# Indirect writes of expert rows: add to the zeroed scratch tensor, or overwrite it

## The chip, the cores and the metric

The kernel runs on one core of one Trainium2 chip. The metric is the device time of one execution in microseconds (us); the lower, the better. The time before is the median of three runs.

## What is computed

The input x holds 16 sequences of 256 tokens with 128 features: 4096 tokens. It is layer-normalised to xn, and the output is x plus two branches of xn: a gated recurrence (a causal convolution of four taps, two sigmoid gates, a scan along the sequence, a projection and an RMS norm) and a mixture of eight experts. Only the second is touched here:

```python
probs = softmax(xf @ Wr);  eidx = argmax(probs);  p_tok = probs[eidx]
rank  = position of the token among those of its expert;  keep = rank < cap    # cap = 4096 / 8 = 512
xe = xf[dispatch]                                   # expert e: its (up to) 512 rows
h  = maximum(einsum('ecd,edf->ecf', xe, W1), 0.0)
ye = einsum('ecf,efd->ecd', h, W2)
ye = ye * (pe * valid)[:, :, None]
y  = zeros((t, d)).at[dispatch.reshape(-1)].add(ye.reshape(E * cap, d))
return x + recurrence(xn) + y
```

Each token has one expert, so a row of y gets at most one row of ye. A token beyond the capacity of its expert gets zero.

## The kernel before

The work is written by hand as one instruction list for each engine, with semaphores between them. It has three stretches.

**Routing.** x is loaded, normalised and written to the scratch tensor `xn_rows` in DRAM (line 296, SP's queue). The router's logits give `idx_in` (which token stands in which expert slot) and `idx_out` (to which row of `y_rows` the result of a slot goes). For a slot without a token `idx_out` names a row of its own in the second half of `y_rows`, which nobody reads. The first half (4096 rows) is filled with zeros by four DMAs on SP's queue (line 300), since the rows of dropped tokens are read later though no slot writes them.

**Experts.** There are 8 experts with 4 tiles of 128 rows each, 32 tiles in all. GpSimd (POOL) issues for each tile a gather (line 366: 128 rows of 512 bytes from `xn_rows` into the tile of `xn_tok`, called `gathered`) and later a scatter (line 373: the 128 result rows of the tile to the rows of `y_rows` that `idx_out` names). POOL's order is `gather(0)` to `gather(3)`, then `scatter(e)` and `gather(e + 4)` in turn for e = 0 to 3, and then `scatter(4)` to `scatter(7)`. `scatter(e)` waits until VectorE (DVE) has copied the expert's output out of PSUM into the same tiles (`evict`, line 940, and tile by tile at line 945 for expert 7). Before its first scatter, POOL waits on `idx_done` and on `zero_out`, which counts the four zero fills. TensorE (PE) transposes the gathered rows (`turn`, line 512), and runs the up products (lines 525 to 527) and the down products (line 538). ScalarE (ACT) and DVE run the recurrence, cut into stages, between the steps of the experts. SP loads the weights of expert e once the gathers of expert e - 2 have landed (line 305).

**End.** SP waits until all 32 scatters have landed (`scattered` at 16 x 32), and issues eight loads of `y_rows` (line 309). ACT or DVE multiplies these rows by the token's probability (lines 719, 988), DVE adds the rest (lines 988, 993), and eight stores on the queues of SP and ACT write the output (lines 312, 724).

Of the kernel before, what the change touches and what calls it, by code (L numbers as in the profile page):

```python
# [9 lines left out]
ALU = mybir.AluOpType  # L10
# [4 lines left out]
B, L, D = 16, 256, 128  # L15
# [28 lines left out]
def rglru_moe_kernel(nc, x, params, gamma, weights, xn_rows, y_rows, out):  # L44
# [14 lines left out]
    with ExitStack() as ctx:  # L59
# [6 lines left out]
        def sem(name):  # L66
            return ctx.enter_context(nc.semaphore(name))
# [63 lines left out]
        gathered = xn_tok  # L131
# [100 lines left out]
        scattered = sem("scattered")  # L232
# [53 lines left out]
        @block.sync  # L286
        def _(sp):
            for u, (t0, nt) in enumerate(UNITS):
                if u not in ACT_UNITS:
                    sp.dma_start(tiles(x_tok, t0, nt), tile_rows(x_rows, t0, nt)).then_inc(x_in[u], 16)  # L290
            for e in range(2):
                sp.dma_start(w_raw[:, e, :], weights[:, e * WW:(e + 1) * WW]).then_inc(w_in[e], 16)
            sp.dma_start(gam[:, :], gamma.partition_broadcast(P)).then_inc(gam_in, 16)
            for u, (t0, nt) in enumerate(UNITS):
                normalised(sp, (t0 + nt) // 4 - 1)
                sp.dma_start(own_rows(xn_rows, t0, nt), tiles(xn_tok, t0, nt)).then_inc(xn_out, 16)

            sp.wait_ge(zeroed, 1)
            for c in range(C):
                sp.dma_start(y_rows[c * TC:(c + 1) * TC, :].rearrange("(p j) d -> p (j d)", p=P),  # L300
                             zeros).then_inc(zero_out, 16)

            for e in range(2, E):
                sp.wait_ge(gather_in[e - 2], 16 * ST)
                sp.dma_start(w_raw[:, e, :], weights[:, e * WW:(e + 1) * WW]).then_inc(w_in[e], 16)

            sp.wait_ge(scattered, 16 * NS)
            for n in range(NH):
                sp.dma_start(tiles(ybuf, 4 * n, 4), own_rows(y_rows, 4 * n, 4)).then_inc(y_in[n], 16)
            for n in range(0, NH, 2):  # L310
                sp.wait_ge(final_done, n + 1)
                sp.dma_start(tile_rows(out_rows, 4 * n, 4), tiles(ybuf, 4 * n, 4)).then_inc(stored, 16)
            sp.wait_ge(stored, 16 * NH)

        @block.gpsimd
        def _(pool):
            g = nc.gpsimd
            exact = dict(allow_small_or_imprecise_dtypes=True)
            g.memset(eps[:, 0:1], LN_EPS).then_inc(eps_done, 1)
            g.memset(eps[:, 1:2], RMS_EPS).then_inc(eps_done, 1)  # L320
            g.memset(eps[:, 2:3], 0.25).then_inc(eps_done, 1)
            g.memset(ident[:, :], 0.0).then_inc(fill, 1)
            g.memset(ones[:, :], 1.0).then_inc(fill, 1)
            g.memset(later[:, :], 0.0).then_inc(fill, 1)
            pool.wait_ge(fill, 1)
            g.affine_select(out=ident[:, :], in_=ident[:, :], compare_op=ALU.not_equal, fill=1.0, base=0,
                            pattern=[[-1, P]], channel_multiplier=1).then_inc(ident_done, 1)

            pool.wait_ge(fill, 3)
            g.affine_select(out=later[:, :], in_=later[:, :], compare_op=ALU.is_ge, fill=-1.0, base=0,  # L330
                            pattern=[[1, P]], channel_multiplier=-1).then_inc(consts, 1)
            g.iota(tok_id[:, :], [[1, NT]], base=-T // 2, channel_multiplier=NT, **exact).then_inc(consts, 1)
            g.iota(block_id[:, :, :], [[P, ST], [0, NT]], base=0, channel_multiplier=0, **exact).then_inc(consts, 1)
            g.iota(slot_in[:, :], [[P, ST]], base=0, channel_multiplier=1, **exact).then_inc(consts, 1)
            g.iota(spare[:, :, :], [[CAP, E], [P, ST]], base=T // 2, channel_multiplier=1,
                   **exact).then_inc(consts, 1)

            def normalise(u):
                t0, nt = UNITS[u]
                pool.wait_ge(nmr_done, u + 1)  # L340
                for t in range(t0, t0 + nt):
                    if t in POOL_TILES:
                        g.tensor_scalar(xn_tok[:, t * D:(t + 1) * D], x_tok[:, t * D:(t + 1) * D], rstd[:, t:t + 1],  # L343
                                        nmr[:, t:t + 1], ALU.mult, ALU.add).then_inc(norm_pool, 1)

            def number(part):
                v0, v1 = part * P // 4, (part + 1) * P // 4
                g.iota(values[:, v0:v1, :], [[1, P // 4], [0, NT]], base=v0, channel_multiplier=0,
                       **exact).then_inc(valued, 1)

            for part in range(4):
                number(part)
            normalise(0)
            normalise(1)
            normalise(2)
            normalise(3)
            pool.wait_ge(par_in, 16)
            pool.wait_ge(ident_done, 1)
            for k in range(TAPS):
                g.tensor_scalar(diag[:, k, :], ident[:, :], par[:, CONV_W + k:CONV_W + k + 1], 0.0, ALU.mult,  # L360
                                ALU.add).then_inc(diag_done, 1)
            normalise(4)

            def gather(e):
                for s in range(e * ST, (e + 1) * ST):
                    g.indirect_dma_start(gathered[:, s * D:(s + 1) * D], None, xn_rows,  # L366
                                         bass.IndirectOffsetOnAxis(ap=idx_in[:, s:s + 1], axis=0)
                                         ).then_inc(gather_in[e], 16)

            def scatter(e):  # L370
                for s in range(e * ST, (e + 1) * ST):
                    pool.wait_ge(y_done, s + 1 if e == E - 1 else ST * (e + 1))
                    g.indirect_dma_start(y_rows, bass.IndirectOffsetOnAxis(ap=idx_out[:, s:s + 1], axis=0),  # L373
                                         gathered[:, s * D:(s + 1) * D], None).then_inc(scattered, 16)

            pool.wait_ge(xn_out, 16 * NU)
            pool.wait_ge(xn_tp, NH)
            pool.wait_ge(idx_done, 1)
            AHEAD = 4
            for e in range(AHEAD):  # L380
                gather(e)
            pool.wait_ge(idx_done, 2)
            pool.wait_ge(zero_out, 16 * C)
            for e in range(E):
                scatter(e)
                if e + AHEAD < E:
                    gather(e + AHEAD)
# [637 lines left out]
```

## Time and profile before

| | us |
|---|---|
| device time, three runs | 145.51, 145.52, 144.76 |
| median | 145.51 |
| span of the profiled execution | 153.7 |
| from the start of the last scatter's issue to the end of that span | 18.6 |

The only time shown of the profiled execution is its span, from the first to the last instruction. It is 8.2 us longer than the median of the runs, which were taken without the profiler; a row of the trace stands for a share of 153.7 us. The page gives the busy time of each engine, then the span in 40 equal slices of 3.84 us, the DMA queues, the chain of work that ended last, and the costliest groups of instructions by line. The bar of an indirect DMA on POOL is the time in which POOL builds the transfer's descriptors; the move of the data comes after it. The timeline gives, in square brackets, how long the engine stood idle before the instruction, and what ended that.

### The profile page before, as it was taken

To read this page: it belongs to the slowest core of one execution; us is meant where nothing else is said; L and a number is where in the kernel's file an instruction comes from. 1 tells how busy PE (TensorE), PEld (TensorE's weight loads), DVE (VectorE), ACT (ScalarE), POOL (GpSimd) and SP (SyncE) were. 2 spreads that over 40 slices of the span, in tenths; PEclk is the share of its full clock that TensorE was granted. 3 is DMA by queue.
4 is the path that set the end of the run, shared out by engine and by line. 5 is a ranking of instruction groups with operands and counts; after the bars stand their busy time and mean duration, and the time that the engine had idled before them with its cause. 6 is when DMAs were issued, how large, how long until landed. Compare 5 with 4: busy or idle time off the path is not lost.

```text
span 153.7 us, 2064 instructions
## 1 busy us (share of the span) xinstructions
PE 111.9 (73%) x676; PEld 89.6 (58%) x676; DVE 96.8 (63%) x213; ACT 91.3 (59%) x207; POOL 87.2 (57%) x104
## 2 busy tenths in 40 slices
PE   5594988990999759979989382999999999400000
PEld 5494976730478437936936272798989979400000
DVE  6474779898699610183143014998989189972770
ACT  3262897561388255948935397484959859620560
POOL 8924570088777737737777720797977746640000
PEclk9999999999599987999999997599999999955555
DMA  3997339711643641115116110001111111117996
GB/s 111 305 339 271 134 143 399 286 32 36 187 116 113 188 143 64 51 34 171 55 51 188 51 34 0 31 25 37 31 48 42 51 36 53 34 34 251 327 337 178
DMA packets 14346, 19.27 MB, mean 125 GB/s; under 512 B 1664, under 2 KB 10112, under 8 KB 14336
## 3 DMA queue, kind: packets, MB, share of 16 engines
q1 hardware_dynamic: 8464, 12.91, 25.7%
q0 software_dynamic: 2048, 4.20, 9.0%
q10 hardware_dynamic: 3824, 2.04, 4.8%
q8 instruction: 5, 0.08, 0.2%
q14 instruction: 5, 0.04, 0.1%
HBM read 10.76 MB, written 8.39 MB: 125 GB/s over the span
## 4 chain that ended last, share of the span: by engine, by line
PE 43%; DMA 15%; ACT 14%; DVE 9%; issue 5%; POOL 4%; another core or an unknown queue 4%; SPq 1%; POOLq 1%; ACTq 1%; DVEq 0%
PE bank L472 10%; DMA x_tok<-in_x 8%; PE bank L538 7%; PE bank L527 5%; PE bank L525 5%; PE bank L526 5%; DMA dec<-y_rows 4%; ACT sq L687 4%; PE bank L404 3%; POOL xn_tok L366 3%; DVE sca L955 2%; PE bank L512 2%; DMA y_rows<-xn_tok,idx_out 2%; DMA xn_tok<-xn_rows,idx_in 2%
## 5 line engine op out<-in xcount | busy, mean ns | idle before, releaser
L373 POOL DMA_INDIRECT y_rows<-xn_tok,idx_out x32 | 36.1, 1128 | 24.1 <-DVE xn_tok L940 14.5
L366 POOL DMA_INDIRECT xn_tok<-xn_rows,idx_in x32 | 36.0, 1125 | 18.0 <-issue 9.4
L538 PE MATMUL bank<-w_raw,h_sb 128*128 128x128 f32 x256 | 30.5, 276 | 2.6 <-issue 1.6
L538 PEld LDWEIGHTS bank<-w_raw,h_sb 128*128 128x128 f32 x256 | 29.4, 192 | 2.9 <-issue 1.8
L674 ACT ACTIVATE h_sb<-bank 128x512 f32<-128x512 f32 x32 | 19.2, 599 | 15.4 <-PE bank L527 11.5
L472 PE MATMUL bank<-xc,par 128*128 128x512 f32 x32 | 17.9, 687 | 4.0 <-ACT dec L649 4.0
L525 PE MATMUL bank<-xg_hi,w_hi 128*128 128x512 f32 x32 | 16.9, 529 | 3.7 <-DVE xg_lo L905 3.6
L871 DVE TENSOR_TENSOR w_lo<-w_raw,w_hi 128x512 fp32r<-128x512 f32 x8 | 5.5, 682 | 15.1 <-issue 13.2
L905 DVE TENSOR_TENSOR xg_lo<-bank,xg_hi 128x512 fp32r<-128x512 f32 x8 | 5.5, 691 | 14.3 <-ACT xg_hi L668 10.5
L527 PE MATMUL bank<-xg_hi,w_lo 128*128 128x512 f32 x32 | 13.7, 430 | 0.0
L526 PE MATMUL bank<-xg_lo,w_hi 128*128 128x512 f32 x32 | 13.7, 429 | 0.0
L472 PEld LDWEIGHTS bank<-xc,par 128*128 128x128 f32 x32 | 6.0, 204 | 11.0 <-issue 10.9
L898 DVE SCALAR_TENSOR_TENSOR xc<-xnT,par,xc 128x1020 f32<-128x1020 f32 (+2 forms) x9 | 11.5, 1277 | 0.3
L525 PEld LDWEIGHTS bank<-xg_hi,w_hi 128*128 128x128 f32 x32 | 7.0, 218 | 7.4 <-DVE xg_lo L905 4.2
L343 POOL TENSOR_SCALAR xn_tok<-x_tok,rstd,nmr 128x128 f32<-128x128 f32 x16 | 7.5, 479 | 6.6 <-DVE nmr L767 6.6
L649 ACT ACTIVATE dec<-bank,half_b 128x512 f32<-128x512 f32 x8 | 5.2, 685 | 9.4 <-PE bank L472 4.6
L687 ACT ACTIVATE sq<-bank 128x128 f32<-128x128 f32 x32 | 8.8, 275 | 1.9 <-PE bank L552 1.2
L719 ACT ACTIVATE dec<-dec,prob 128x128 f32<-128x128 f32 x16 | 5.1, 391 | 8.1 <-DMA dec<-y_rows 8.0
L933 DVE TENSOR_TENSOR_SCAN xnT<-dec,inp 128x256 f32<-128x256 f32 x16 | 9.7, 672 | 0.0
L955 DVE SCALAR_TENSOR_TENSOR sca<-bank,rms,gam 128x128 f32<-128x128 f32 x32 | 9.0, 345 | 0.3
L922 DVE SCALAR_TENSOR_TENSOR inp<-inp,xc 128x512 f32<-128x512 f32 x8 | 5.2, 692 | 5.5 <-ACT inp L649 5.5
L526 PEld LDWEIGHTS bank<-xg_lo,w_hi 128*128 128x128 f32 x32 | 7.0, 219 | 2.7 <-issue 1.5
(118 smaller groups left out, 212.4 us busy)
## 6 DMA issues: line engine op xcount, KB each, us to landing
w_raw<-in_weights SPq DMA_DIRECT2D x8, 512.0 KB, 9.0
y_rows<-sca SPq DMA_DIRECT2D x4, 512.0 KB, 4.9
dec<-y_rows SPq DMA_DIRECT2D x8, 256.0 KB, 4.9
xn_rows<-xn_tok SPq DMA_DIRECT2D x3, 512.0 KB, 2.6
x_tok<-in_x SPq DMA_DIRECT2D x2, 512.0 KB, 7.5
out<-dec SPq DMA_DIRECT2D x4, 256.0 KB, 3.6
out<-dec ACTq DMA_DIRECT2D x4, 256.0 KB, 3.5
x_tok<-in_x ACTq DMA_DIRECT2D x1, 512.0 KB, 12.0
```

Of the source, the lines that this page charges most:

```text
L366: g.indirect_dma_start(gathered[:, s * D:(s + 1) * D], None, xn_rows, bass.IndirectOffsetOnAxis(ap=idx_in[:, s:s + 1], axis=0)).then_inc(g ...
L373: g.indirect_dma_start(y_rows, bass.IndirectOffsetOnAxis(ap=idx_out[:, s:s + 1], axis=0), gathered[:, s * D:(s + 1) * D], None).then_inc(s ...
L472: mm(gate[n % 2][:, :], par[:, w:w + D], xc[:, c * TC + (i % 2) * HT:c * TC + (i % 2 + 1) * HT], start=True, stop=True).then_inc(gate_mm, 1)
L525: mm(b, w_hi[:, e % 2, w], xg_hi[:, :], start=True, stop=False)
L526: mm(b, w_hi[:, e % 2, w], xg_lo[:, :], start=False, stop=False)
L527: mm(b, w_lo[:, e % 2, w], xg_hi[:, :], start=False, stop=True).then_inc(h_mm, 1)
L538: last = mm(tile_of(e, s), h_sb[:, k * CAP + s * P:k * CAP + (s + 1) * P], w_raw[:, e, F + k * D:F + (k + 1) * D], start=(k == 0), stop=(k ...
L674: a(h_sb[:, k * CAP:(k + 1) * CAP], hbank[n % 3][:, :], ACT.Relu).then_inc(h_done, 1)
L687: a(sq[:, :], obank[n % 3][:, i * D:(i + 1) * D], ACT.Square, accum_out=ssq[:, t:t + 1]).then_inc(ssq_done, 1)
L898: ins = v.scalar_tensor_tensor(dst[:, :, back:], src[:, :, 0:L - back], par[:, k:k + 1], dst[:, :, back:], ALU.mult, ALU.add)
L933: last = v.tensor_tensor_scan(hs[:, o:o + L], dec[:, o:o + L], inp[:, o:o + L], 0.0, ALU.mult, ALU.add)
L955: v.scalar_tensor_tensor(attn[:, t * D:(t + 1) * D], obank[n % 3][:, i * D:(i + 1) * D], rms[:, t:t + 1], gam[:, :], ALU.mult, ALU.mult).t ...
```

## The change

The scatter of line 373 gets `compute_op=ALU.add`: each of its 128 rows is added to what stands in `y_rows`, where it overwrote it before. The rows that are read later were zero, and `idx_out` names no row twice, so the first half of `y_rows` holds the same numbers. No instruction is added, removed or moved on any engine, and no wait is changed.

```diff
                 for s in range(e * ST, (e + 1) * ST):
                     pool.wait_ge(y_done, s + 1 if e == E - 1 else ST * (e + 1))
                     g.indirect_dma_start(y_rows, bass.IndirectOffsetOnAxis(ap=idx_out[:, s:s + 1], axis=0),
-                                         gathered[:, s * D:(s + 1) * D], None).then_inc(scattered, 16)
+                                         gathered[:, s * D:(s + 1) * D], None,
+                                         compute_op=ALU.add).then_inc(scattered, 16)
```

## Rows read from the trace of the kernel before

**Rows 1.** The page: span, engines' busy time, and slices for POOL and DMA
```profile
span 153.7 us, 2064 instructions
PE 111.9 (73%) x676; PEld 89.6 (58%) x676; DVE 96.8 (63%) x213; ACT 91.3 (59%) x207; POOL 87.2 (57%) x104
...
POOL 8924570088777737737777720797977746640000
...
DMA  3997339711643641115116110001111111117996
```

**Rows 2.** Chain that ended last, in time order: start us, us, what
```profile
130.82 0.41 DVE xn_tok L945 x2
131.23 0.07 issue
131.30 0.96 POOL y_rows L373
132.26 1.27 POOLq L59
133.52 0.30 issue
133.83 0.96 POOL y_rows L373
134.79 0.30 issue
135.09 2.69 DMA y_rows<-xn_tok,idx_out
137.80 0.33 SPq L309
```

**Rows 3.** The two indirect DMAs in the page's groups: busy, mean ns, idle before
```profile
L373 POOL DMA_INDIRECT y_rows<-xn_tok,idx_out x32 | 36.1, 1128 | 24.1 <-DVE xn_tok L940 14.5
L366 POOL DMA_INDIRECT xn_tok<-xn_rows,idx_in x32 | 36.0, 1125 | 18.0 <-issue 9.4
```

**Rows 4.** Line 373 by itself: duration min/median/max, first and last start
```profile
L373 POOL DMA_INDIRECT y_rows<-xn_tok,idx_out x32: 957/977/2626, 56.1 to 135.1; - x32
```

**Rows 5.** POOL's timeline: start us, us, instruction, idle before it
```profile
68.57 1.18 POOL L373 DMA_INDIRECT y_rows<-xn_tok,idx_out  x1 [2.59 <-DVE xn_tok L940]
...
96.33 1.18 POOL L373 DMA_INDIRECT y_rows<-xn_tok,idx_out  x1 [6.96 <-DVE xn_tok L940]
...
108.88 2.65 POOL L366 DMA_INDIRECT xn_tok<-xn_rows,idx_in  x1 [0.30 <-issue]
111.83 1.48 POOL L373 DMA_INDIRECT y_rows<-xn_tok,idx_out  x1 [0.30 <-issue]
...
121.72 0.96 POOL L373 DMA_INDIRECT y_rows<-xn_tok,idx_out  x1 [0.30 <-issue]
124.81 0.96 POOL L373 DMA_INDIRECT y_rows<-xn_tok,idx_out  x1 [2.13 <-DVE xn_tok L940]
...
131.30 0.96 POOL L373 DMA_INDIRECT y_rows<-xn_tok,idx_out  x1 [1.42 <-DVE xn_tok L945]
...
135.09 1.42 POOL L373 DMA_INDIRECT y_rows<-xn_tok,idx_out  x1 [0.30 <-issue]
```

**Rows 6.** The chain at the first gather that PE waits for
```profile
35.98 2.54 DMA xn_tok<-xn_rows,idx_in
```

**Rows 7.** The same gather in POOL's timeline
```profile
35.98 1.01 POOL L366 DMA_INDIRECT xn_tok<-xn_rows,idx_in  x1 [0.30 <-issue]
```

**Rows 8.** PE's timeline: the transposes of expert 7's gathered rows
```profile
117.97 0.60 PE L512 MATMUL bank<-ident,xn_tok 128*128 128x128 f32 x4
```

**Rows 9.** Engines and DMA share from 96.3 to 122.7 us (12 scatters, 4 gathers)
```profile
96.30:122.70 26.40, 26.20 (x181) 23.99 (x180) 22.29 (x44) 18.92 (x56) 21.77 (x16) 0.92 0.13 39
```

**Rows 10.** What SP's queue waited for
```profile
SPq L309 <- DMA y_rows<-xn_tok,idx_out: 56.7, 1, 56.7
```

**Rows 11.** The zero fills of line 300, and their landing
```profile
L300 SPq DMA_DIRECT2D y_rows<-sca x4: 424/984/1184, 22.7 to 25.2; - x4
...
DMA to landing us min/median/max: 3.6/4.9/5.8
```

**Rows 12.** SP's weight loads (first and last start), and ACT's use of expert 7's
```profile
L305 SPq DMA_DIRECT2D w_raw<-in_weights x6: 327/328/333, 38.5 to 80.8; - x6
...
117.77 0.62 ACT L627 ACTIVATE w_hi<-w_raw 128x512 fp32r<-128x512 f32 x1
```

## Prediction

> **What bounds the kernel now.** I read the page first. No engine is busy for more than 73% of the span, and POOL's row of slices shows it at work in nearly every slice up to the 36th and empty after it, while DMA rises to 9 tenths [rows 1]. So the kernel has an end in which only transfers and a little arithmetic are left, and it cannot start before something has happened. The chain of waits, in order of time, says what: DVE's copies of expert 7's output, two issues of line 373 on POOL with the queue between them, the last transfer into y_rows, and then SP's loads of y_rows [rows 2]. SP had stood at that wait for 56.7 us [rows 10]. The end from 137.80 to 153.7 us, 15.9 us, is the same work after the change, so all that counts is when the last scatter lands.
>
> The second thing to see is how much room POOL has. One line-373 instruction takes 0.98 us in the median [rows 4], and 0.30 us pass before the next, so a back-to-back scatter costs POOL 1.28 us. Both kinds of indirect DMA stand at a mean of 1.13 us [rows 3], since some are stretched, up to 2.65 us. The idle times ahead of each group of scatters are the slack: 2.59 us before scatter(1), none before scatter(2), 6.96 us before scatter(3) at 96.33, none before scatter(4) and scatter(5), 2.13 us before scatter(6) at 124.81, and 1.42 us before scatter(7) at 131.30 [rows 5]. From 96.33 us on POOL is thus nearly as slow as the rest of the kernel: 20 of the 32 scatters are issued there with 3.55 us of slack in all.
>
> **What the change costs, step by step.** Nothing moves, and no wait is added; the wait for the zero fills was there already, and they had landed by 31.0 us (25.2 + 5.8) [rows 11], 25 us before the first scatter at 56.1 us [rows 4]. What changes is each scatter, in two terms.
>
> Term 1, the issue on POOL. Call d what one instruction of line 373 gets longer. The trace has no adding DMA. From below d is 0: same rows, same indices, one instruction; the trace shows no work in it that the addition would save, so I see no gain. From above I take d = 0.98 us: a row now needs its target read as well, and the nearest rows for naming 128 more rows are a whole second indirect instruction. Between these: a plain scatter reads once and writes once for each row, an adding one reads twice and writes once. If the whole 0.98 us goes with the number of such accesses, d is a half of it, 0.49 us; if half of the instruction is fixed, d is 0.24 us. Gather and scatter take the same time though the indexed side is another [rows 3], which speaks for a cost by the count of accesses or a fixed one and not for a cost of the indexed side. I take the middle, d = 0.37 us.
>
> How d reaches the end: before 96.33 us the slack takes it all. Scatter(1) starts on time while 4d is below 2.59, and scatter(3) while 8d is below 6.96 (with d = 0.37: 1.48 and 2.96). From 96.33 us, 12 scatters (experts 3, 4, 5) stand ahead of scatter(6): 12 x 0.37 = 4.44, less 2.13 of slack, makes it start 2.31 us late. Its own four add 1.48, less 1.42 of slack: scatter(7) starts 2.37 us late. The last four add 1.48: 3.85 us. In general the sum is 4d while 16d is below 3.55, that is below d = 0.22, and 20d - 3.55 us above it.
>
> Who else stands behind these issues? gather(7), behind scatter(3), comes 4d = 1.48 us later. It ended its issue at 111.53 us [rows 5]; a gather lands 1.53 us after its issue (2.54 - 1.01) [rows 6, 7], so at 113.1 before and 114.5 now, and PE wants it at 117.97 [rows 8]. This cover is gone only at d = 1.2 us. SP's last weight load, which waits for gather(5), goes out at 80.8 us, and ACT wants expert 7's weights at 117.77 [rows 12]. So PE, ACT and DVE go on as before, and the term is POOL's alone: 3.85 us.
>
> Term 2, the last landing. The last scatter lands 1.29 us after its issue has ended (2.69 - 1.42, and 0.02 to SP) [rows 2, 5]. Adding needs a read of DRAM ahead of the write. From below this costs nothing, from above a whole gather in series, 1.53 us [rows 6, 7]. A gather, which does read DRAM, lands only 0.24 to 0.26 us later than a scatter; the transfers themselves need 0.13 x 26.4 / 16 = 0.21 us of each DMA engine [rows 9], and a second read could double that. I take 0.5 us.
>
> A rule on the transfer itself: The Trainium skill (Collectives: The Full Stack, Why ReduceScatter is half of AllGather) says that adding in the DMA's path costs no time by itself but needs two read descriptors for each piece, so that the rate is about halved. By that, an estimate of 0.43 us per transfer where the row has 0.21, still far below the 1.28 us between two issues; it would change only term 2, by 0.2 us, which is within what I took.
>
> Sum: 3.85 + 0.5 = 4.35 us. The profiled span is 8.2 us above the median of the runs, so its rows are if anything too long (by 5%, 0.2 us of this sum); I leave that out. 145.5 + 4.35 = 149.9 us.
>
> **Rivals.**
> (a) The issue stays as it is, d below 0.15. For it: the 0.98 us may be nearly all fixed, and no row here divides it. Then the slack hides all but the last four issues: 4d, at most 0.6, and term 2 of 0 to 1.5 us. The time is 145.5 to 147.6, most likely 146.0. That the addition is not done at all and the transfer is a plain write would look the same, at 145.5.
> The Trainium skill (DMA: Bandwidth & Descriptors, Where the ~2 µs actually goes) speaks for this rival: it calls the generation of descriptors small, and says that many can be emitted before their cost shows. No row here can test it, since all 64 indirect DMAs have 128 rows.
> (b) The issue costs twice as much or more, d of 0.65 or above. Then POOL is the bound already before 96.33 us: with d = 0.98, scatter(1) starts 1.33 us late, scatter(3) is 1.33 + 7.84 - 6.96 = 2.2 us late, and the end is 2.2 + 16.05 + 0.5 = 18.8 us later, at 164.3. PE then waits for gather(7) too (2.2 + 3.9 against 4.9 us of cover), which POOL's lateness contains. At d = 0.65 it is 9.45 + 0.5, 155.5. For it: an adding form may be built by a slower path, and what stretches the issue at 108.88 to 2.65 us while others take 0.96 could weigh on more accesses as well.
> (c) The transfers pile up on the DMA engines. Each engine has 8 rows of a scatter; if it finishes read, add and write of one before the next begins, at 0.3 us each (the 0.26 us that a read adds, and a little), a transfer takes 2.4 us where POOL issues one each 1.28 us. That works like d = 1.1 us: some 20 us more, 165 or later. It decides only once a transfer takes 6 times its 0.21 us [rows 9], and the slices show DMA at 1 tenth there [rows 1].
> (d) Faster. The adding form is built otherwise, and its issue isn't stretched as the last one is, 1.42 against 0.96 us [rows 5]: 0.46 us; and its landing wait shrinks since rows are confirmed in another way. It needs the 1.29 us to fall under about 1.0 to count: 144.7 us. Shorter issues elsewhere give nothing, since scatter(6) and scatter(7) wait for DVE. Nothing in the trace points to it.
>
> **How the numbers follow.** What a measurement of this kernel can tell from no change is about 0.5%, 0.7 us: 144.8 to 146.2. Forecast (d of 0.15 to 0.65: 146.4 to 155.5): 0.47. Rival (a): 0.27, of which 0.21 within 0.5% and 0.06 slower. Rival (b): 0.17. Rival (c): 0.06. Rival (d): 0.03. Slower: 0.47 + 0.06 + 0.17 + 0.06 = 0.76. Same 0.21, faster 0.03. For the range, 145.6 leaves out (d) and the lowest edge of (a), some 0.06, and 160 leaves out (c) and the part of (b) with d above 0.85, some 0.14. The sum's own steepness makes it wide: above d = 0.22 each 0.1 us in one issue is 2 us at the end.
>
> **What would show it.** The row of line 373: a median of 1.35 us where it has 0.98 says that term 1 is right, 0.98 says (a), 1.95 says (b). POOL's idle time before scatter(6) and scatter(7) should be gone, and before scatter(3) fall from 6.96 to about 4.0. The last transfer should land 1.8 us after its issue's end and not 1.3. The row of line 366 should not change, PE should find gather(7) in place, and the stretch from SP's first load to the end should stay at 15.9 us. I am wrong if line 373 is unchanged and the end still comes late (then it is the transfers), or if PE or SP's weight loads begin to wait for gathers.

## The result

| | median, us | lowest to highest | runs |
|---|---|---|---|
| kernel before | 145.51 | 144.76 to 145.68 | 4 |
| changed kernel | 157.38 | 156.69 to 158.49 | 4 |

The medians differ by 11.9 us, a ratio of 1.082. The comparison's own ratio is 1.0897 (95% interval 1.0841 to 1.0953), some 13 us of 145.5. Here and below a ratio compares only the faster executions of both kernels and a difference in us compares the medians of all, so the two can differ by about 1%. The forecast was 149.9 us with a range of 145.6 to 160.0. The direction was right, the size was 4.4 us where 11.9 came.

The profile of the changed kernel, from its page: span, busy times, slices, and the groups and DMA rows of the indirect transfers (its lines from 373 on stand one or more higher than before).

```profile
span 155.1 us, 2064 instructions
PE 110.5 (71%) x676; PEld 89.9 (58%) x676; DVE 96.5 (62%) x213; ACT 91.4 (59%) x207; POOL 103.2 (67%) x104
...
POOL 8924760187778688788788879887888888850000
...
DMA  4996349511652655238217412322342444436997
...
q0 software_dynamic: 5632, 4.20, 20.1%
...
POOL 55%; issue 14%; DMA 12%; PE 5%; DVE 4%; ACT 4%; POOLq 1%; ACTq 1%; DVEq 0%; SPq 0%
...
L373 POOL DMA_INDIRECT y_rows<-xn_tok,idx_out x32 | 53.1, 1660 | 10.1 <-issue 10.1
L366 POOL DMA_INDIRECT xn_tok<-xn_rows,idx_in x32 | 35.0, 1094 | 18.0 <-issue 9.4
```

Line 373 took POOL 36.1 us before [rows 3] and takes 53.1 us now. All its idle time is "issue", 0.3 us between two instructions: no scatter waits for VectorE any more. POOL holds 55% of the chain that ended last. The same line by itself (duration min/median/max, first and last start), and the last step of the chain in time order (start us, us, what), to be held against [rows 4] and [rows 2]:

```profile
L373 POOL DMA_INDIRECT y_rows<-xn_tok,idx_out x32: 1542/1557/2102, 54.0 to 136.5; - x32
```
```profile
134.65 1.55 POOL y_rows L373
136.20 0.30 issue
136.50 3.26 DMA y_rows<-xn_tok,idx_out
139.76 0.02 issue
139.78 0.33 SPq L309
```

The median instruction grew from 0.977 to 1.557 us, and the landing after the end of the last issue from 1.27 to 1.71 us (3.26 - 1.55; 2.69 - 1.42 before).

One number in these spans does not fit the forecast's working: 153.7 us before and 155.1 us after differ by 1.4 us, and the runs by 11.9. In the changed kernel a run's time is 1.8 us above the span of the same execution (156.89 and 155.1). So an execution of 153.7 us span would be a run of some 155.5 us, 10 us above the median of the kernel before. This suggests that the trace that the prediction read was not of an execution like the timed ones; the first experiment looks at that.

### The profile page after: what moved, and what is told of

It reads as the page before. It is cut to its first block, busy times and chain, and to the rows that moved or that the text cites. A ratio compares the mean times of both kernels' runs of the same rounds, so it can differ in the third digit from the quotient of the medians.

```text
span 155.1 us, 2064 instructions
## 1 busy us (share of the span) xinstructions
PE 110.5 (71%) x676; PEld 89.9 (58%) x676; DVE 96.5 (62%) x213; ACT 91.4 (59%) x207; POOL 103.2 (67%) x104
## 3 DMA queue, kind: packets, MB, share of 16 engines
q0 software_dynamic: 5632, 4.20, 20.1%
## 4 chain that ended last, share of the span: by engine, by line
POOL 55%; issue 14%; DMA 12%; PE 5%; DVE 4%; ACT 4%; POOLq 1%; ACTq 1%; DVEq 0%; SPq 0%
POOL y_rows L373 32%; POOL xn_tok L366 22%; DMA x_tok<-in_x 7%; DMA dec<-y_rows 2%; DMA y_rows<-xn_tok,idx_out 2%; ACT xn_tok L595 2%; DVE dec L989 2%; PE bank L499 1%; ACT xnT L604 1%; POOLq L59 1%; PE bank L437 1%; DVE dec L994 1%; DVE stats L758 1%; ACT dec L720 1%; PE bank L417 1%
## 5 line engine op out<-in xcount | busy, mean ns | idle before, releaser
L373 POOL DMA_INDIRECT y_rows<-xn_tok,idx_out x32 | 53.1, 1660 | 10.1 <-issue 10.1
L366 POOL DMA_INDIRECT xn_tok<-xn_rows,idx_in x32 | 35.0, 1094 | 18.0 <-issue 9.4
L539 PE MATMUL bank<-w_raw,h_sb 128*128 128x128 f32 x256 | 29.9, 275 | 0.0
L526 PE MATMUL bank<-xg_hi,w_hi 128*128 128x512 f32 x32 | 15.2, 476 | 3.4 <-DVE xg_lo L906 3.3
L473 PE MATMUL bank<-xc,par 128*128 128x512 f32 x32 | 16.5, 639 | 0.0
L989 DVE SCALAR_TENSOR_TENSOR dec<-dec,prob,x_tok 128x128 f32<-128x128 f32 x16 | 4.5, 344 | 14.5 <-DMA dec<-y_rows 14.5
L528 PE MATMUL bank<-xg_hi,w_lo 128*128 128x512 f32 x32 | 13.0, 408 | 0.0
L526 PEld LDWEIGHTS bank<-xg_hi,w_hi 128*128 128x128 f32 x32 | 6.3, 197 | 6.2 <-DVE xg_lo L906 3.9
L405 PE MATMUL bank<-w_router,dec 128*128 128x128 f32 x64 | 9.3, 295 | 0.0
L513 PE MATMUL bank<-ident,xn_tok 128*128 128x128 f32 x32 | 5.4, 294 | 5.4 <-DMA xn_tok<-xn_rows,idx_in 5.4
```

The costliest lines, as they stand in the source:

```text
L405: last = mm(bank[6][:, t * E:t * E + D], xT[:, t * P:(t + 1) * P], w_router[:, :], start=True, stop=True)
L473: mm(gate[n % 2][:, :], par[:, w:w + D], xc[:, c * TC + (i % 2) * HT:c * TC + (i % 2 + 1) * HT], start=True, stop=True).then_inc(gate_mm, 1)
L526: mm(b, w_hi[:, e % 2, w], xg_hi[:, :], start=True, stop=False)
L528: mm(b, w_lo[:, e % 2, w], xg_hi[:, :], start=False, stop=True).then_inc(h_mm, 1)
L539: last = mm(tile_of(e, s), h_sb[:, k * CAP + s * P:k * CAP + (s + 1) * P], w_raw[:, e, F + k * D:F + (k + 1) * D], start=(k == 0), stop=(k ...
```

## The experiments

**The kernel before, profiled again.** No edit.

> The kernel before, unchanged, profiled once more. In the trace of the changed kernel the runs lie 1.8 us above the span (156.89 and 155.1), so the 153.7 us trace of the kernel before may be of an execution some 10 us longer than its runs of 145.5 us. Theory A (that trace was not typical): a span of about 143.7 us, DVE's copies of the experts' outputs at about 52.5, 62.8, 72.6, 85.5, 94.5, 103.6, 113.5 and 121.4 us as in the changed kernel, and POOL's idle time ahead of the scatters at about 0, 0, 0, 1.6, 0, 1, 5 and 2 us for experts 0 to 7. Rival B (the profiler lengthens this kernel): a span near 153.7 us again, with idle times of 2.8, 2.6, 0, 7.0, 0, 0, 2.1 and 1.4 us.

145.06 us (143.59 to 145.67, 11 runs) beside 144.71 for the same kernel in the same set. The profiled execution took 143.59 us with a span of 141.8. From its page, its line-373 row, POOL's timeline (only the instructions that follow an idle time of over 0.31 us; the last number is that idle time) and the end of the chain:

```profile
span 141.8 us, 2064 instructions
...
q0 software_dynamic: 2048, 4.20, 10.1%
```
```profile
L373 POOL DMA_INDIRECT y_rows<-xn_tok,idx_out x32: 952/972/2634, 53.7 to 122.9; - x32
```
```profile
53.73 0.99 POOL L373 DMA_INDIRECT y_rows<-xn_tok,idx_out  x1 [0.60 <-issue]
...
85.11 1.18 POOL L373 DMA_INDIRECT y_rows<-xn_tok,idx_out  x1 [0.75 <-DVE xn_tok L940]
...
111.95 0.95 POOL L373 DMA_INDIRECT y_rows<-xn_tok,idx_out  x1 [1.97 <-DVE xn_tok L940]
...
119.15 0.95 POOL L373 DMA_INDIRECT y_rows<-xn_tok,idx_out  x1 [2.15 <-DVE xn_tok L945]
```
```profile
122.93 2.72 DMA y_rows<-xn_tok,idx_out
125.65 0.02 issue
125.67 0.33 SPq L309
```

Theory A held: the span is 141.8 us where it wanted 143.7, and the idle times stand in its places except before expert 5. Its sizes were too large before experts 3, 5 and 6 (0.75, 0 and 1.97 us where it wanted 1.6, 1 and 5). The profiler does not lengthen the kernel by 8 us. In the execution of the prediction the other engines were late: the copy of expert 3's output was at 95.37 us, where it is at 84.14 us here. So POOL waited for them. Its idle times were 2.59 + 6.96 + 2.13 + 1.42 = 13.1 us between the first and the last scatter [rows 5] (and 2.8 us before the first); here they are 0.75 + 1.97 + 2.15 = 4.87 us. Each of them also holds the 0.30 us that pass between two instructions that wait for nothing. What a longer issue can use up, the slack, is smaller by that: 11.9 us there, 3.97 us here. (In two more traces, of the kernel with overwriting scatters of half the width and of the kernel in which only the last scatter adds, the idle times are 1.39, 1.98 and 2.14, and 0.67, 2.01, 1.94 and 2.14: a slack of 4.6 and 5.6 us.)

Two things set the late execution apart. ScalarE and VectorE stood until 54.6 us for something that the trace calls "remote" and does not name:

```profile
54.58 1.27 ACT L649 ACTIVATE dec<-bank,half_b 128x512 f32<-128x512 f32 x2 [3.81 <-remote]
54.60 0.69 DVE L940 COPY xn_tok<-bank 128x512 f32<-128x512 f32 x1 [2.11 <-remote]
```

And TensorE's granted clock fell more often. Three windows of that trace, then the same three of this one (length, busy time of PE, PEld, DVE, ACT and POOL with their instructions, granted clock as a share of full speed, DMA share, GB/s):

```profile
40.00:45.00 5.00, 5.00 (x15) 3.00 (x15) 4.89 (x5) 2.85 (x5) 3.84 (x4) 0.74 0.50 151
55.00:60.00 5.00, 4.59 (x10) 2.68 (x11) 0.29 (x1) 2.57 (x5) 2.97 (x4) 0.66 0.42 133
95.00:100.00 5.00, 5.00 (x12) 3.93 (x13) 5.00 (x9) 1.97 (x4) 3.06 (x3) 0.50 0.08 26
```
```profile
40.00:45.00 5.00, 5.00 (x18) 3.11 (x17) 4.89 (x5) 4.32 (x7) 3.77 (x5) 1.00 0.42 141
55.00:60.00 5.00, 5.00 (x41) 4.61 (x40) 1.07 (x2) 4.38 (x6) 3.87 (x4) 1.00 0.50 157
95.00:100.00 5.00, 5.00 (x42) 4.80 (x41) 5.00 (x9) 4.65 (x19) 4.17 (x3) 1.00 0.11 26
```

PE was busy for 111.9 us there and for 107.1 us here with the same 676 instructions. The 0.50 is the lower of the clock's two levels (1.2 of 2.4 GHz); PE had been busy for only 1.76 us from 90 to 95 us, ahead of it. This trace has one low stretch of its own, 0.73 from 85 to 90 us. What starts the difference stays open. The kernel before had a median of 144.7, 145.5 and 145.3 us in three further sets of its runs and 153.2 us in a fourth, and its trace of 153.7 us fits that one: a kernel profiled in that fourth set, the one with fewer gathers and the addition below, has the same stall, 3.76 us before 54.27 us, and no other trace of these kernels has it.

**Half of the scatters add.** The edit is against the changed kernel.

```diff
-                                         compute_op=ALU.add).then_inc(scattered, 16)
+                                         compute_op=ALU.add if e < 4 else ALU.bypass).then_inc(scattered, 16)
```

> Only the 16 scatters of experts 0 to 3 add, the other 16 overwrite. Theory A (POOL's issue is 0.58 us longer, and POOL has almost no slack before expert 3 in a typical execution): POOL comes 9 us later to expert 3's scatters, less 1.6 us of slack there, and some 6 us of slack later on take most of it: about +1.5 to +2 us, 147.3 us. Rival B (the slack of the prediction, 2.6 and 7.0 us ahead of scatters 1 and 3): everything is absorbed, 145.5 us.

148.85 us (148.79 to 150.08, 4 runs), ratio 1.0373 (1.0234 to 1.0511): +4.1 us. This is neither expectation. With the slack that the new trace shows it should be 16 x 0.585 - 3.97 = +5.4 us; in this kernel's trace the last scatter starts 5.2 us later than in the kernel before (128.13 against 122.93). Rival B, the slack of the prediction, would have hidden all of it.

The other half, with `e >= 4`:

> Only the 16 scatters of experts 4 to 7 add. Theory A: POOL runs through scatters 4 and 5, has slack left before scatter 6, and the last four add 4 x 0.58 and 0.4 us of landing: about +2.8 us, 148.3 us. Rival B (slack of 2.1 and 1.4 us only): 16 x 0.58 - 3.55 + 0.4 = +6.1 us, 151.6 us.

152.03 us (151.63 to 153.14, 4 runs), ratio 1.0558 (1.0435 to 1.0681): +7.3 us. That is above both and close to rival B's number, 151.6, though not for rival B's reason. In the two traces the first scatter of expert 4 starts at 102.81 us here and at 100.09 in the kernel before, and the last of all at 131.85 and 122.93. So 2.7 us had been lost ahead of any adding scatter, and the stretch with them is 6.2 us longer (29.04 against 22.84). The 15 issues in it take 9.7 us more than the plain ones, since five of them took 1.67 to 1.95 us and not 1.55, and the slack in it was 1.97 + 2.15 - 2 x 0.30 = 3.5 us: 6.2 us. The 2.7 us are a difference between two executions, which the medians may contain as well.

**POOL held up without any addition.** The edit is against the kernel before; the lines that declare the tile and the semaphore are left out.

```diff
...
+                    if s > 0:
+                        pool.wait_ge(filled, s)
+                    g.iota(filler[:, :], [[1, 448]], base=0, channel_multiplier=0, **exact).then_inc(filled, 1)
```

> All scatters overwrite, as before, and POOL fills a scratch tile of 448 half-precision numbers per partition after each of them (no effect on the output), which should take 0.5 to 0.6 us of POOL. Theory A (the loss is POOL's issue time): +9.5 to +11 us, 155 to 156.5 us. Rival C (the loss is in the adding transfers: more packets, a read of DRAM for each row): no more than +1 us, 146.5 us.

151.22 us (150.62 to 152.2, 4 runs), ratio 1.0534 (1.0397 to 1.067): +6.5 us. Its POOL timeline, for two scatters of the last group:

```profile
127.59 0.97 POOL L375 DMA_INDIRECT y_rows<-xn_tok,idx_out  x1 [0.17 <-issue]
128.56 0.53 POOL L379 IOTA filler<- 128x448 f16 x1
129.25 0.96 POOL L375 DMA_INDIRECT y_rows<-xn_tok,idx_out  x1 [0.17 <-issue]
```

The filler takes 0.53 us, but the gap before the next scatter shrinks, so the scatters follow each other every 1.66 us where they did every 1.26: 0.40 us more, not 0.55 as meant. 31 x 0.40 - 3.97 = 8.4 us, and in the trace the last scatter starts 8.0 us later (130.93 against 122.93); the medians differ by 6.5. So Theory A's 155 to 156.5 us was missed, by 4 us, because the filler was too short for it. Rival C's 146.5 us was missed as well, on the other side: time on POOL's queue alone, with plain transfers, costs several us. What this run cannot show is that the adding transfers cost nothing besides; for that see the rows with half the width and the run with one adding scatter.

**What an issue is made of.** Four kernels with smaller scatters: 64 rows, or 128 rows of half the width, overwriting and adding.

```diff
-                    g.indirect_dma_start(y_rows, bass.IndirectOffsetOnAxis(ap=idx_out[:, s:s + 1], axis=0),
-                                         gathered[:, s * D:(s + 1) * D], None,
+                    g.indirect_dma_start(y_rows, bass.IndirectOffsetOnAxis(ap=idx_out[0:64, s:s + 1], axis=0),
+                                         gathered[0:64, s * D:(s + 1) * D], None,
```

> All scatters overwrite, but each writes only the 64 rows of partitions 0 to 63; the other half of the expert rows is left out of the output. It divides the 0.97 us of a plain line-373 instruction. Theory P (the time goes with the rows): about 0.50 us. Rival F (it is fixed for each instruction): 0.97 us. In between, 0.97 = fixed + 128 x r, with r read from here.

> The same with adding scatters of 64 rows. The 128-row instruction took 1.56 us, 0.58 more than the plain one. Theory P (the addition costs 4.6 ns for each row, on POOL): 0.29 us above the plain one of 64 rows. Rival F (a fixed 0.58 us, another path in the same instruction): 0.58 us above it. By P POOL has room again and the time is near or below that of the kernel before, 143 to 145.5 us; by F about 147 to 149 us.

> All scatters overwrite with 128 rows of 256 bytes in place of 512: only the first 64 features of a row are written, and to other places of the scratch tensor, so half of the expert rows is left out. If the issue is for descriptors and not for bytes, the instruction stays at 0.97 us; if for bytes, it falls towards 0.5 us.

> Adding scatters of 128 rows of 256 bytes (the same part left out). If the 0.58 us belong to descriptors, the instruction stays at 1.56 us and the time at about 156 to 157 us; if to bytes, it falls to about 1.27 us or less, and the time to about 150 us.

The line-373 rows of the four (64 rows plain, 64 rows adding, half width plain, half width adding; each from its own trace):

```profile
L373 POOL DMA_INDIRECT y_rows<-xn_tok,idx_out x32: 892/905/2065, 52.5 to 121.7; - x32
```
```profile
L373 POOL DMA_INDIRECT y_rows<-xn_tok,idx_out x32: 1392/1404/1879, 54.2 to 133.6; - x32
```
```profile
L373 POOL DMA_INDIRECT y_rows<-xn_tok,idx_out x32: 957/962/1493, 54.4 to 124.8; - x32
```
```profile
L373 POOL DMA_INDIRECT y_rows<-xn_tok,idx_out x32: 1546/1552/1986, 54.1 to 136.2; - x32
```

| scatter, median of one | 64 rows | 128 rows | per row | what is left at no rows |
|---|---|---|---|---|
| overwrites | 0.905 us | 0.972 us | 1.05 ns | 0.84 us |
| adds | 1.404 us | 1.557 us | 2.39 ns | 1.25 us |
| difference | 0.499 us | 0.585 us | 1.34 ns | 0.41 us |

The last column draws a line through two points. Both rivals are near the truth in one part: of the 0.585 us of a full scatter some 0.41 us come with the instruction and 0.17 us with its rows. The width plays no part (1.552 against 1.557, 0.962 against 0.972). The times go with the issues: 142.77, 153.84, 144.96 and 157.48 us (of 2, 2, 8 and 2 runs) beside 145.51 for the kernel before in the same set. Halving the rows gives only 3.6 us of the 12 back (157.48 to 153.84), so theory P, which wanted the time back at that of before, falls. Theory F's 147 to 149 us were missed too: 32 x (1.404 - 0.972) - 3.97 = 9.9 us by the corrected slack, 8.3 measured. The half width also bears on the transfers: q0 was busy for 16.9% of 154.8 us, 26.2 us, where it had 31.2 us in the changed kernel, and neither the issue nor the time went down with it.

**POOL relieved, with the addition left in.**

```diff
-                sp.wait_ge(gather_in[e - 2], 16 * ST)
+                sp.wait_ge(gather_in[min(e - 2, 3)], 16 * ST)
...
-                if e + AHEAD < E:
-                    gather(e + AHEAD)
...
-                pe.wait_ge(gather_in[e], 16 * ST)
+                pe.wait_ge(gather_in[min(e, 3)], 16 * ST)
```

> All 32 scatters add as in the changed kernel, but the 16 gathers of experts 4 to 7 are left out (their transposes read the normalised tokens that stand in those tiles, so the output of these experts is not the reference's), and SP's last two weight loads wait for gather(3) in place of gathers 4 and 5. That takes some 22 us from POOL's queue and nothing from the adding transfers. Theory A (POOL's queue is the bound): POOL has idle time ahead of most scatters again, only the last four and their landing still cost 3 x 0.58 + 0.1 + 0.4 us: about 147.5 us. Rival C (the adding transfers, or DRAM reads of them, hold the end back): 156 us or more, as in the changed kernel.

> The same without the addition (all scatters overwrite; the same part is left out). In the kernel before, POOL has 4.9 us of idle time between its first and its last scatter, and the last group waits for VectorE. Both theories: no change beyond 0.5 us, 144.5 to 145.5 us; it is the base for the run with the addition.

151.51 us with the addition (149.15 to 153.09, 4 runs) and 145.92 without (144.89 to 147.69, 4 runs). This is the set in which the kernel before stood at 153.2 us. The two differ by 5.6 us, where the changed kernel had +11.9 with the same adding transfers, so about half of the loss went with 16 instructions on POOL that do not add, and rival C's 156 us or more falls. One thing here was expected by nobody: the kernel without the addition is 7.3 us faster than the kernel before in the same set (ratio 0.9521, 0.9456 to 0.9586), and at the 145 us of the other sets. Either taking the gathers out also takes out what makes 153 us, or these runs happened to miss it; that stays open, and it makes the 5.6 us less sure. Between the two profiled executions the difference is 5.4 us, of which 1.5 us stood before expert 3's scatters (90.91 against 89.37 us, with the stall of 3.76 us in the one trace only) and 3.0 us came on POOL after them. Theory A wanted +2.4 us, and the traces show part of why it is more. Three rows of POOL's timeline of the kernel with the addition, and the same place of the one without:

```profile
90.91 1.74 POOL L373 DMA_INDIRECT y_rows<-xn_tok,idx_out  x1 [5.83 <-DVE xn_tok L939]
...
100.03 2.63 POOL L373 DMA_INDIRECT y_rows<-xn_tok,idx_out  x1 [0.30 <-issue]
102.97 3.22 POOL L373 DMA_INDIRECT y_rows<-xn_tok,idx_out  x1 [0.30 <-issue]
```
```profile
98.23 2.29 POOL L373 DMA_INDIRECT y_rows<-xn_tok,idx_out  x1 [1.29 <-DVE xn_tok L938]
...
107.25 0.96 POOL L373 DMA_INDIRECT y_rows<-xn_tok,idx_out  x1 [1.44 <-DVE xn_tok L938]
...
116.25 0.96 POOL L373 DMA_INDIRECT y_rows<-xn_tok,idx_out  x1 [3.90 <-DVE xn_tok L938]
```

POOL has its idle times back up to expert 3, but from 90.91 us on the adding scatters follow each other without a pause to the end: seven issues of 1.74 to 3.22 us up to 108.6 us use up the room. An issue of 1.55 us in the median was 1.74 us in the mean in that trace. VectorE runs its scans from 91.75 to 106.5 us there; that they stretch the issues was not tested.

**One scatter adds, the last.** The edit is `if s == NS - 1`.

> Only the very last scatter adds. Theory A: its own issue, 0.58 us, and its landing, 0.43 us later after the issue has ended (1.71 against 1.28), so +1.0 us against the kernel before at the same level; in the trace 3.2 to 3.3 us from its start to the landing where the kernel before had 2.7. Rival C (adding transfers are slow by themselves): more than +2 us.

146.58 us (145.56 to 147.56, 12 runs) beside 145.25 (17 runs), ratio 1.0092 (1.0059 to 1.0126): +1.3 us. In its trace the last issue took 2.09 us where it had 1.44, though no other adding transfer was under way, and the landing came 1.72 us after it:

```profile
125.09 3.81 DMA y_rows<-xn_tok,idx_out
128.90 0.02 issue
128.92 0.33 SPq L309
```

The end is 1.1 us later than in the kernel before (3.81 against 2.72), of which 0.44 us are the landing; from start to landing 3.2 to 3.3 us were expected. The interval of the times, 0.9 to 1.8 us, holds that and leaves no room for an adding transfer that is slow by 2 us.

**The changed kernel again.** No edit.

> The changed kernel once more, beside the kernel before. The kernel before stood at 144.7 and 145.5 us in two sets of runs and at 153.2 us in a third, so its own time has two levels 8 us apart. Theory A (at either level the changed kernel is held by POOL's queue, which is full from the first gather on, so whatever delays the other engines by 8 us costs it little): 156 to 158 us at either level, that is +12 us if the kernel before shows 145, and +4 to +5 us if it shows 153. Rival D (the 8 us are added to both): 157 beside 145, 165 beside 153.

159.08 us (156.11 to 160.6, 6 runs) beside 145.25 us; the profiled execution, of 157.2 us, has line 373 at a mean of 1.658 us and once more no wait for VectorE. The median is 1 us above the 156 to 158 us of theory A, and the difference is 13.8 us. The kernel before stood at its lower level in this set, so whether the changed kernel is slower at the upper level too was not seen. That POOL's queue would hide a lateness of the others stays an expectation.

No run pointed to a version that beats both kernels: the smaller scatters cost nearly as much on POOL as full ones, and the faster runs left out a part of the output.

## Why the prediction came out too small

**What bounds the kernel, and the mechanism: right.** The end starts when the last scatter has landed; the change lengthens POOL's instruction, POOL's queue carries it to the end, and no other engine matters. In the changed kernel POOL has no stop of over 0.31 us between its first and its last scatter. The filler showed that POOL's time alone costs, the kernel with fewer gathers that relief on POOL takes about half of the loss away.

**Term 1, the size of d: too small.** Taken as 0.37 us, measured 0.58. The step that failed is the split of the 0.98 us. It was assumed to be for the most part a cost for each access to a row, half of it or all. The runs with 64 rows show that 0.84 of the 0.97 us do not depend on the rows, and that the addition brings another fixed 0.41 us, which neither of the bounds had as such. By the prediction's own formula the right d gives 20 x 0.58 - 3.55 = 8.05 us and not 3.85, which is 4.2 of the 7.5 us that were missing.

**Term 1, the slack: the wrong execution.** The sum subtracted POOL's idle times as that trace had them, and let the 12 scatters before 96.33 us cost nothing. The traces of ordinary executions have 4.0 to 5.6 us of slack in all, and all 32 scatters count. A smaller slip goes the same way: the prediction counts 0.30 us between two instructions as part of a scatter's 1.28 us and then subtracts the whole of each idle time, which holds the 0.30 us too, so its 3.55 us of slack were 2.95. The sums of POOL's timeline in the two comparable traces close the account:

| us | kernel before, profiled again | changed kernel | difference |
|---|---|---|---|
| first scatter starts | 53.73 | 54.01 | +0.3 |
| 31 scatter issues before the last | 33.4 | 51.6 | +18.2 |
| 16 gather issues among them | 17.5 | 16.6 | -0.9 |
| the 0.30 us between two instructions, 47 times | 14.3 | 14.3 | 0.0 |
| idle time above 0.30 us | 4.0 | 0.0 | -4.0 |
| last scatter, start to landing | 2.72 | 3.26 | +0.5 |
| from there to the end | 16.1 | 15.3 | -0.8 |
| span | 141.8 | 155.1 | +13.3 |

The medians of the runs gave 11.9 us and, in a second set, 13.8. This is where the other 3.3 us of the 7.5 are. The sentence that failed is "The profiled span is 8.2 us above the median of the runs, so its rows are if anything too long (by 5%)". A span longer than the runs was taken for a scale, though the execution had stalls in it: the waits called "remote" were in the trace, 3.8 and 1.5 us at ScalarE and 2.8 us at VectorE, and so was the clock. Idle time on the engine in question is just what lateness of the others makes.

**Term 2: right.** 0.5 us forecast, 0.43 measured (1.71 against 1.28). Its reason was half wrong: the time on the DMA engines did not double, it more than tripled. Queue q0 was busy for 20.1% of 155.1 us, 31.2 us, where it had 10.1% of 141.8, 14.3 us: 0.53 us more for each adding transfer on each DMA engine, on top of 0.22. The Trainium skill's rule of two reads and half the rate (Collectives: The Full Stack, Why ReduceScatter is half of AllGather) gives, as the prediction's estimate from its row of 0.21 us, 0.43 us in all where 0.75 was seen, so this trace goes beyond it. The longer transfer stayed without visible effect: POOL gives out one each 1.85 us.

**The others in POOL's queue: nearly right.** SP's weight loads held no one up. PE did wait for gather(7), for 1.52 us before 109.13 us, which the prediction had excluded for d below 1.2 us; it wanted the rows earlier than in the trace that was read, and POOL was late by then. It cost nothing, since PE finished at 123.3 us, 13 us before the last scatter was issued. By the prediction's own signs a wait of PE for gathers meant that it was wrong; it was a sign of the larger d and not of another mechanism.

**The rivals.** (a), an issue that stays as it is, was excluded by the first row. The Trainium skill's sentence for it (DMA: Bandwidth & Descriptors, Where the ~2 µs actually goes), that many descriptors can be emitted before their cost shows, is borne out for rows, at 1 to 2.4 ns each. Its "small" is not borne out here: the fixed part is 0.84 us for a plain scatter, and the adding one costs 0.41 us more before the first row. (b), d of 0.65 or more, was missed by 0.07 us, and its warning that POOL would be the bound before 96.33 us came true already at 0.58. (c) did not happen: 0.75 us on a DMA engine against 1.85 us between two issues. (d) did not either.

## What to carry to other kernels

An indirect DMA is mostly a fixed price on POOL, here some 0.84 us and 0.30 us to the next, and adding in it raises the 0.84 to 1.25 us (drawn from 64 and 128 rows): where POOL's queue has little slack, an addition that "the transfer does on the way" is paid by the issuing engine. Before slack is subtracted from a sum, check that the profiled execution is like the timed ones; where its span is longer than the runs, look for waits that the trace does not name, compare TensorE's granted clock, and take the slack once with them and once without. From an idle time take off what passes between two instructions in any case. With 32 instructions in one queue, count how often the price is paid before asking how large it is.

## What the runs showed of the hardware

An adding indirect scatter makes a packet for each row, an overwriting one does not. The 64 indirect DMAs of the kernel before make 2048 packets on q0, 32 each (1536 for the 48 of the kernel with fewer gathers), and it is 2048 again with scatters of 64 rows or of 256-byte rows. With the addition it is 5632, 112 more for each of the 32 scatters, so 144 each; with 64 rows 3584, so 80 each; with rows of 256 bytes 5632 again. That is one for each row and 16 more.

The same kernel stood at 144.7 to 145.5 us in three further sets of its own runs and at 153.2 us in another, on one chip both at 145.5 and at 153.2 in two sets, with a spread of 2.7 to 3.9 us within a set. The mean granted clock does not tell the levels apart: 0.899 to 0.931 at the lower, 0.892 to 0.925 at the upper. A comparison is safe only within a set, and even there one kernel can show a level that another does not.
